# The bf16 split of the first attention's queries and keys on GpSimd and ScalarE in place of VectorE

## The reference, cut to what matters

```python
def qkv(h):
    t = (h @ qkv_W).reshape(b, n, 3, H, HD)          # H = 16 heads, HD = 8
    q, k, v = (t[:, :, 0], t[:, :, 1], t[:, :, 2])
    return (_apply_rope(q, cos, sin), _apply_rope(k, cos, sin), v)
...
s = jnp.einsum('bqhd,bkhd->bhqk', q, k) * scale
s = jnp.where(mask, s, jnp.finfo(s.dtype).min)
a = jax.nn.softmax(s, axis=-1)
return jnp.einsum('bhqk,bkhd->bqhd', a, v)
```

## Time and profile before

| | before |
|---|---|
| median of 3 runs | 969.55 us (968.15 to 973.97) |
| the profiled execution | 973.68 us |
| its span, first to last instruction | 971.8 us |
| TensorE busy | 909.4 us, 94% of the span |
| VectorE busy | 704.0 us, 72% |
| ScalarE busy | 550.3 us, 57% |
| GpSimd busy | 147.1 us, 15% |
| mean granted TensorE clock | 0.973 of full speed |

### The profile page before, as it was taken

The page is one execution under the profiler, slowest core; times in us unless marked ns, Lnnn a source line. Parts: engine busy times, 40 slices in busy tenths (PEclk is TensorE's granted clock), DMA queues, the critical chain, the costliest instruction groups (busy, mean ns, idle before and its releaser), DMA issues.

```text
span 971.8 us, 15418 instructions
## 1 busy us (share of the span) xinstructions
PE 909.4 (94%) x4959; PEld 396.5 (41%) x4986; DVE 704.0 (72%) x1933; ACT 550.3 (57%) x1033; POOL 147.1 (15%) x388
## 2 busy tenths in 40 slices
PE   3858999999999999999999999999899999999998
PEld 3523344334434345444444544434333334334443
DVE  5598958978887758643464667798599898886752
ACT  5023565465555566683437362377576676676773
POOL 1013200003000022210111120022001102021210
PEclk9877999999999999999999999999899999999999
DMA  8042131012311202000020224012422140004201
GB/s 312 29 134 66 54 110 29 18 42 75 86 59 49 60 3 69 3 8 1 1 66 7 66 91 111 7 56 80 103 66 60 46 115 24 3 3 135 81 3 33
DMA packets 66323, 57.49 MB, mean 59 GB/s; under 512 B 19407, under 2 KB 63427, under 8 KB 65988
## 3 DMA queue, kind: packets, MB, share of 16 engines
q1 hardware_dynamic: 64996, 54.73, 19.6%
q10 hardware_dynamic: 1248, 1.77, 0.5%
HBM read 31.01 MB, written 24.49 MB: 57 GB/s over the span
## 4 chain that ended last, share of the span: by engine, by line
PE 80%; DVE 12%; issue 3%; ACT 2%; DMA 1%; POOL 0%; SPq 0%; ACTq 0%; DVEq 0%
PE pv_bank L1540 15%; PE bank L1518 11%; PE bank L1495 10%; PE bank L1520 5%; PE bank L1522 4%; DVE bank L1271 3%; PE bank L1651 3%; PE bank L1646 3%; PE bank L1498 3%; PE bank L1633 3%; PE bank L1599 2%; PE bank L1600 2%; PE bank L1565 2%; PE bank L1506 2%; PE bank L1468 2%
## 5 line engine op out<-in xcount | busy, mean ns | idle before, releaser
L1019 ACT ACTIVATE pr<-bank 128x512 f32<-128x512 f32 (+1 forms) x704 | 371.3, 600 | 148.4 <-PE bank L1520 56.9
L1271 DVE CUSTOM_DVE_ANT_0 bank<-bank,mask_q 128x512 f32<-128x512 f32 x256 | 170.5, 718 | 24.6 <-PE bank L1495 23.3
L1274 DVE TENSOR_REDUCE mx<-bank 128x1 f32<-128x512 f32 x256 | 161.8, 684 | 32.9 <-PE bank L1495 32.3
L1518 PE MATMUL bank<-qs,ks 103*128 103x512 bf16 x512 | 178.6, 387 | 4.5 <-DMA qs<-mrow 2.3
L1495 PE MATMUL bank<-ks,qs 97*128 97x512 bf16 x512 | 166.2, 394 | 10.0 <-issue 7.5
L1540 PE MATMUL pv_bank<-pr,va 128*32 128x512 f32 x1024 | 137.3, 608 | 0.2
L1276 DVE TENSOR_REDUCE mx<-bank 128x4 f32<-128x308 f32 x192 | 81.5, 469 | 19.1 <-PE bank L1498 18.3
L915 POOL CAST mp<-mx 128x16 bf16<-128x16 f32 x80 | 16.4, 205 | 516.0 <-DVE mx L1271 203.5
L1518 PEld LDWEIGHTS bank<-qs,ks 103*128 103x128 bf16 x512 | 46.5, 98 | 117.3 <-ACT pr L1019 39.5
L1520 PE MATMUL bank<-mask_k,identb 128*128 128x512 bf16 x229 | 87.6, 383 | 0.0
L1495 PEld LDWEIGHTS bank<-ks,qs 97*128 97x128 bf16 x512 | 47.3, 99 | 98.8 <-issue 29.6
(11 more groups left out here) (219 smaller groups left out, 1186.8 us busy)
## 6 DMA issues: line engine op xcount, KB each, us to landing
qs<-q_parts SPq DMA_DIRECT2D x40, 384.0 KB, 4.6
q_parts<-xn SPq DMA_DIRECT2D x20, 384.0 KB, 2.6
ks<-k_parts SPq DMA_DIRECT2D x64, 96.0 KB, 2.6
q_parts<-xn SPq DMA_DIRECT2D x20, 256.0 KB, 2.2
k_parts<-u SPq DMA_DIRECT2D x8, 384.0 KB, 2.4
q_parts<-u SPq DMA_DIRECT2D x20, 128.0 KB, 2.1
qs<-mrow SPq DMA_DIRECT2D x160, 6.0 KB
late<-late_w SPq DMA_DIRECT2D x1, 2432.0 KB, 13.0
```

The lines of the kernel that those rows point to most:

```text
L1019: act.activation(pr[0:K, 4 * (group % NSLOT) + t % 4, :], bank(k)[0:K, :], ACT.Exp, scale=SCALE).then_inc(act_done, 1)
L1271: dve.tensor_tensor_reduce(b[:, :], b[:, :], mask_q[:, qb, :], 1.0, -3e38, ALU.add, ALU.max, dst[:, qb, g, e:e + 1]).then_inc(dve_done, 1)
L1274: dve.tensor_reduce(dst[:, qb, g, e:e + 1], b[:, :], AX.X, ALU.max).then_inc(dve_done, 1)
L1518: ins = pe.matmul(b[:, :], ks[s][0:ROWS, e, g, kb * P:(kb + 1) * P], qs[s][0:ROWS, g, :], start=True, stop=(a != 0))
```

## The change: what is done where

For attention 0 the one step `parts` on VectorE becomes three steps: `rest` on GpSimd (q - part 1 into `r1`), `second` on ScalarE (cast of `r1` to part 2), `third` on GpSimd (`r1` - part 2 into part 3). `parts_out` waits for `third`. Every step that writes into `hid` (VectorE's `rope` and `parts`, ScalarE's `proj` of layer 1, `gate_h`, `mlp_h`) now also waits for the last `third` ahead of it in the plan. The other attentions keep their `parts`. The scheduler knows the new steps and their holds, and its bonuses have other values, so the whole order is another one. The core of the diff:

```diff
-    "part1": ("act",), "parts": ("dve",), "part1_out": ...
+    "part1": ("act",), "parts": ("dve",), "rest": ("pool",), "second": ("act",), "third": ("pool",), "part1_out": ...
 def split(s, a, w):
     return (of(s, ("part1", a, w)) + (of(s, ("part1_out", a)) if w == 0 else [])
-            + of(s, ("parts", a, w), ("parts_out", a, w)))
+            + of(s, ("rest", a, w), ("second", a, w), ("third", a, w), ("parts_out", a, w)))
...
-TABLE_LOAD, TABLE_KEPT = 1.3, -143.9017
+TABLE_LOAD, TABLE_KEPT = 1.3, -149.7069
...
-EAGER = {"chain": 0.401623, "rows": 0.078331, "max": 0.046568, "exp": 0.072625, "pv": -0.094903, "tables": 0.309366}
+EAGER = {"chain": 0.401744, "rows": 0.045653, "max": 0.045471, "exp": 0.141877, "pv": -0.093953, "tables": 0.155199}
...
+                def rest(k, s, a, w):
+                    pool.wait_ge(act_done, count("act", (s, "part1", a, w)))
+                    pool.tensor_tensor(r1[w][s][:, :], qf[w][s][:, :], qpart(w, s, 0), ALU.subtract).then_inc(pool_done, 1)
+
+                def third(k, s, a, w):
+                    pool.wait_ge(act_done, count("act", (s, "second", a, w)))
+                    pool.wait_ge(pool_done, count("pool", (s, "rest", a, w)))
+                    pool.tensor_tensor(qpart(w, s, 2), r1[w][s][:, :], qpart(w, s, 1), ALU.subtract).then_inc(pool_done, 1)
...
+                def second(k, s, a, w):
+                    act.wait_ge(pool_done, count("pool", (s, "rest", a, w)))
+                    act.activation(qpart(w, s, 1), r1[w][s][:, :], ACT.Identity).then_inc(act_done, 1)
...
                     reader = before_in_plan(k, None, "parts")
                     if reader:
                         dve.wait_ge(dve_done, count("dve", reader))
+                    turned = before_in_plan(k, None, "third")
+                    if turned:
+                        dve.wait_ge(pool_done, count("pool", turned))
...
-                    if a == 0:
-                        dve.wait_ge(act_done, count("act", (s, "part1", a, w)))
-                        do(dve.tensor_tensor(rest, qf[w][s][:, :], part[0], ALU.subtract))
```

More of the change, by code:

```diff
@@ L90 @@
     "rope": ("pe", "dve"), "proj": ("pe", "act"), "v": ("pe", "act"),
-    "part1": ("act",), "parts": ("dve",), "part1_out": ("sp",), "parts_out": ("sp",), "stack": ("sp",),
+    "part1": ("act",), "parts": ("dve",), "rest": ("pool",), "second": ("act",), "third": ("pool",), "part1_out": ("sp",), "parts_out": ("sp",), "stack": ("sp",),
     "max": ("pe", "dve"), "max_parts": ("pool",), "max_t": ("pe", "dve"), "max_rows": ("sp",),
@@ L211 @@
          "ln_stats": (1.45,), "ln_rstd": (1.05,), "ln_norm": (1.07,), "ctx_stats": (2.,), "ln_t": (.44, .7),
-         "ctx_norm": (2.5,), "rope": (.86, .82), "part1": (.56,), "parts": (1.85,), "v": (.89, .6), "ctx_t": (.25, .7),
+         "ctx_norm": (2.5,), "rope": (.86, .82), "part1": (.56,), "rest": (1.3,), "second": (.56,), "third": (1.3,), "parts": (1.85,), "v": (.89, .6), "ctx_t": (.25, .7),
          "ctx_k": (.8, .8), "gate_cols": (.3,), "ctx_v": (.88, 1.9), "gates": (.4, .5), "ctx_split": (1.62,), "max_parts": (1.1,),
@@ L333, in before @@
             return [me("act", "ln_t", MLP_LN[rest[0]])], []
+        if kind == "rest":
+            return [me("act", "part1", *rest)], []
+        if kind == "second":
+            return [me("pool", "rest", *rest)], []
+        if kind == "third":
+            return [me("act", "second", *rest)], []
+        if kind == "parts_out":
+            return [me("dve", "parts", *rest) if rest[0] else me("pool", "third", *rest)], []
         if kind in ("part1", "part1_out", "parts"):
@@ L361, in before @@
                   "ln_rstd": ("dve", "ln_stats", *rest), "ln_norm": ("pool", "ln_rstd", *rest),
-                  "parts_out": ("dve", "parts", *rest),
                   "heads_t": ("act", "pv_out", *rest), "attn_t": ("dve", "heads_t", *rest, 1),
@@ L498 @@
 SIMPLE = {"e2_out", "gates", "ctx_k", "ctx_v", "ctx_split", "ctx_out", "ln_rstd", "ln_norm",
-          "parts_out", "heads_t", "attn_t", "mlp_out", "mlp_add", "l1_exp", "l1_probs", "l1_probs_t", "l1_evidence",
+          "heads_t", "attn_t", "mlp_out", "mlp_add", "l1_exp", "l1_probs", "l1_probs_t", "l1_evidence",
           "router", "router_exp", "router_probs", "probs_t", "gate_h", "expert_h", "gate", "l1_add", "store"}
@@ L839, in parts_out @@
                 def parts_out(k, s, a, w):
-                    sp.wait_ge(dve_done, count("dve", (s, "parts", a, w)))
+                    if a == 0:
+                        sp.wait_ge(pool_done, count("pool", (s, "third", a, w)))
+                    else:
+                        sp.wait_ge(dve_done, count("dve", (s, "parts", a, w)))
                     if w == 0:
@@ L998, in hid_free @@
                         act.wait_ge(dve_done, count("dve", reader))
+                    turned = before_in_plan(k, None, "third")
+                    if turned:
+                        act.wait_ge(pool_done, count("pool", turned))
                 def proj(k, s, a, w):
@@ L1248, in parts @@
                         dve.wait_ge(dve_done, count("dve", reader))
-                    if a == 0:
-                        dve.wait_ge(act_done, count("act", (s, "part1", a, w)))
-                        do(dve.tensor_tensor(rest, qf[w][s][:, :], part[0], ALU.subtract))
-                    else:
-                        first = (s, "proj", a, w)
-                        dve.wait_ge(act_done, count("act", first))
-                        b = 0.0 if QBIAS[a] is None else cols[:, QBIAS[a] + w:QBIAS[a] + w + 1]
-                        do(dve.scalar_tensor_tensor(rest, bank(first)[:, :], b, part[0], ALU.add, ALU.subtract))
+                    turned = before_in_plan(k, None, "third")
+                    if turned:
+                        dve.wait_ge(pool_done, count("pool", turned))
+                    first = (s, "proj", a, w)
+                    dve.wait_ge(act_done, count("act", first))
+                    b = 0.0 if QBIAS[a] is None else cols[:, QBIAS[a] + w:QBIAS[a] + w + 1]
+                    do(dve.scalar_tensor_tensor(rest, bank(first)[:, :], b, part[0], ALU.add, ALU.subtract))
                     do(dve.tensor_copy(part[1], rest))
```

4 lines of the change are left out of this document (2 added, 2 removed), and 6 rows, old and new, of the table URGE.

## The result

The changed kernel takes 977.61 us (median of 18 runs, 974.98 to 980.83), the kernel before 971.56 in the same comparison (18 runs, 967.51 to 977.61). The ratio is 1.006, 95% interval 1.0045 to 1.0075: about 6 us slower, where I had forecast 3.2 us faster. The measured time lies just above my range.

What follows compares the result with a forecast made beforehand. TensorE was taken as the bound, 98% busy from 100 to 575 us, with VectorE busiest in the ramp. Ramp gains of 0.3, 1.9 and 1 us made 3.2: 969.55 to 966.3 us, range 957 to 976.

Steps and rivals of the forecast that it cites:

- The prices of the parts: Eight splits: VectorE loses 14.6 us; each GpSimd pass takes 1.28 us, the ScalarE cast 0.63.
- the 78 to 83: Sign of being right, in the ramp: the first `exp` starts at 78 to 83 us.
- my 25.7: Ramp: the way from the first `max` matmul, laid out at 55.6 us, to the first `exp` at 81.3.
- 31 said: Sign of being right: TensorE idle about 31 us in the first 100 us.
- the rival of the held queue: `rope` waiting for `third` holds VectorE's queue, 1.6 us at eight places: 12.8 us, result 982; chance 0.07.
- mutual blocking as I priced it: Rival: all 16 GpSimd passes hit a VectorE instruction at 0.95 us, 15.2 less the 3.2: 981.5; chance 0.05.
- VectorE's time did not count in full: Judges the rival that VectorE, full in the ramp, gives back all 14.6 us: 955; chance 0.20.
- Behind 100 us I take zero: After the ramp: no gain or loss counted, though another order of later layers can add or save a few us.
- The last of my signs of being wrong: A difference that arises behind 100 us and is larger than that of the ramp.
- nothing to be seen: Rival: the ramp's gain is lost at a later place of the new order: 969.5; chance 0.18.
- The 3.2 us of the ramp: Total gain forecast from the start of the kernel: 3.2 us faster.
- the terms of 0.3, 1.9 and 1 us: Ramp: earlier first `exp` 0.3; context keys, values and gates done before it 1.9; maxima running ahead 1.

Runs made afterwards that it cites:

- e5: Step order of the kernel before, with the eight splits on GpSimd and ScalarE, each begun right behind part 1; 0.9993 to the kernel before.
- e2: The changed kernel's step order, with the eight splits put back on VectorE; 1.0053 to the kernel before.
- e14: The changed kernel, order untouched, lane 2's first 16 masked maxima run over half the keys (part of the computation left out); 1.0049 to the kernel before.
- e6: The changed kernel, with GpSimd's 3.51 us memsets for lanes 1 and 2 moved from `ctx_norm` to the start; 1.0085 to the kernel before.
- e10: The changed kernel's engines, lane 0's k rope right behind its q rope, a newly searched order behind it; 1.0018 to the kernel before.
- e12: Kernel before's order with new engines and early splits, first 149 steps rewritten so lane 0's k rope follows its q rope; 0.9822, median 953.45 us.
- e8: The changed kernel, lane 0's last row of maxima moved ahead, two groups of lane 1 and 2 steps placed later; 1.0048 to the kernel before.

## Why the prediction was wrong

**What held.** The prices of the parts: GpSimd's passes took 1.15 us (I had 1.28; my 1.2 to 1.4 lay just above), the cast 0.63, VectorE lost 14.0 us (14.6; its total of 690.0 lies in the 688 to 692). Two more signs came true by luck. The first `exp` at 82.66 lies in the 78 to 83, but only because the first `max` came 4.3 us later than I had laid out and the way from there took 22.7 us in place of my 25.7. TensorE's idle time in the first 100 us is 30.3 (31 said), but its matmuls were slower there, so that hardly more work was done (46.3 us lost against 46.7). VectorE waited for GpSimd ahead of no cos or sin product, so the rival of the held queue fell. So did that of mutual blocking as I priced it: GpSimd's 16 passes took 1151 to 1162 ns each, and of the VectorE instructions that ran beside one of them, mostly masked maxima (at most 733 ns), none was longer than its usual. None of the two products and the sum of a rope ever stood beside a pass, so of these the trace says nothing. VectorE's time did not count in full; it counted for nothing, as TensorE's 98% said. This much of the reading, that TensorE is the bound and eight splits off VectorE are worth little, fits e5.

**The step that failed** is "Behind 100 us I take zero". The hand-over at 140 us alone costs 5 to 6 us, and 300 to 575 us another 1 to 4. The last of my signs of being wrong, a difference that arises behind 100 us and is larger than that of the ramp, is what came. I had seen that the bonuses change and that the order behind the ramp is another, wrote that this can add or save a few of the 28 us of idle time, and gave it no term, no sign and no place. The order was there to be read: nine maxima of lane 2 ahead of lane 0's last one, and the last `exp` tiles of the group before issued among the first four of them. e2 shows that this order costs 0.5% with the old engines too. A last row costs about 8 us from its last maximum to the `exp` (135.9 to 144.1), and TensorE's list has 3.8 us less than that of other work at this place. The rival "nothing to be seen" had the mechanism (the gain lost at a later place of the new order) and stopped at zero, where nothing says that such a loss stops at the size of the gain.

**The 3.2 us of the ramp** were not there either in the profiled pair: 46.3 us lost in the first 100 against 46.7. I laid the start out with old durations. Lane 0's last `third` ends at 51.8, not 47.3, and the first `max` is at 59.9, not 55.6. 0.7 of these 4.3 us is `rstd`, 1.92 us in place of 1.0 since the mask cast now runs beside it:

```profile
22.90 1.22 DVE L1142 TENSOR_SCALAR mask_q<-qs 128x2048 bf16<-128x2048 uint8 x1
```

```profile
23.07 1.92 POOL L925 TENSOR_TENSOR rstd<-var,eps_pow 128x4 f32<-128x4 f32 x1 [18.84 <-DVE var L1241]
```

The rest is TensorE's pace: I had put the q rope's start at 29.7 and the anchors at 4.4 us, and they came out at 32.31 and 6.8, with 0.72 us for each pair of the bias rows. It need not be the order's doing. In e14, which has the same instructions in the same order up to there, the same matmuls ran faster:

```profile
27.96 0.51 PE L1417 MATMUL bank<-early,pr 128*128 128x128 f32 x2
...
32.30 1.62 PE L1425 MATMUL bank<-cond,pr 128*128 128x4 f32 x14
```

There the k rope starts at 37.09 in place of 42.78 and the first `exp` at 77.25 in place of 82.66. So a ramp laid out from one execution is uncertain by 5 us for this alone, and the terms of 0.3, 1.9 and 1 us in my sum were smaller than that. In e14 and e6 the first 100 us lose 40.5 and 43.7 us, 3 to 6 less than before: a gain of the size that I forecast does occur, in the traces whose clock first rises at 28.1 and 37.3 us in place of 47.2. Of the 5.4 us between their first `exp` the spans of e14 and the changed kernel keep at most 2 (974.1 against 976.1).

**The range** ended at 976, and the measured 977.61 is 1.6 above it. The median of before also went up, from 969.55 in the 3 runs that I had to 971.56 in 18; on my base the ratio of 1.006 gives 975.4. So that the number lies outside is due as much to the base as to the forecast, and that the range nearly held the slowdown is luck, as nothing in my sum provided for one. What was wrong is the sign. A term for one missed hand-over, about 6 us, belonged there; that idle time can cost clock as well could be seen in the earlier trace rows, 0.51 and 0.50 of full speed in the two stretches where TensorE was busy for 1.09 and 2.81 of 5 us.

## What to carry to other kernels

When an edit comes with a new schedule, they are two changes: freeze the old order around the new engines, and the new order around the old ones, before either gets the credit. Where one engine is full and its order fixed, follow the last producer of each group: see what stands ahead of it in every queue that it crosses, and how much work that is free to run the full engine has until the result arrives. A gain at the start is kept only if the order behind it is one that had been good; e10 and e12 have much the same early start (first `exp` at 66.7 and 68.0 us), and their medians are 972.7 and 953.5 us, 958.0 when e12 was run again.

## What the runs showed of the hardware that I had not expected

**Matmuls of one kind at two paces, by execution.** The same fp32 matmul pairs of the bias rows followed each other at 0.72 us in the changed kernel and at 0.42 in e14, with a granted clock of 1.00 shown for both stretches (28 to 32 us). In each trace the first record of the clock is its first rise: at 47.2 us in the changed kernel, 28.1 in e14, 31.2 in the kernel before. Until then the views show 1.00, and the matmuls run slowly: the anchors' pairs take 0.52 us in the changed kernel under a shown 1.00, just as in e14 under a shown 0.50 (from 35 us on). So at the start of an execution the granted clock in the rows does not tell the pace. Why the rise came so late in some executions the traces do not show. The Trainium skill, "TensorE: Matmul & The Clock Gate", section "What's actually happening", says that the number of slow matmuls at a start varies from run to run and costs less than 1% of a typical span. The two traces agree: they are 5.4 us apart at the first `exp`, of 976.

**Blocking does occur, but not at the maxima that I feared for.** A VectorE cast of 128x77 took 1.56 us beside GpSimd's memset (0.20 otherwise), and GpSimd's `rstd` 1.92 beside VectorE's mask cast (1.01 otherwise). Both VectorE instructions are `tensor_scalar` with one SBUF operand; the maxima, which read PSUM, were not slowed. The passes of the split can do it too, where the order puts them beside such a cast, as in e5:

```profile
51.35 1.16 POOL L944 TENSOR_TENSOR hid<-hid,u 128x512 f32<-128x512 f32 x1 [14.89 <-ACT u L1062]
51.57 0.99 DVE L1232 TENSOR_SCALAR cmaskf<-cmask 128x77 f32<-128x77 uint8 x1
```

And the collision of the earlier trace rows occurs again in the changed kernel, in a later attention, whose `parts` stay on VectorE (0.69 us otherwise):

```profile
590.97 1.32 POOL L950 TENSOR_TENSOR x<-x,bias_b 128x512 f32<-128x512 f32 x1
591.21 1.63 DVE L1287 TENSOR_TENSOR u<-hid,xn 128x512 bf16<-128x512 f32 x1
```

The Trainium skill, "SBUF — State Buffer", section "Who interferes with whom", names copies, casts and `tensor_scalar` as those that can take the ports shared with GpSimd, and says that whoever came first makes the other wait. The traces agree in both directions: in e8 the cast came behind the memset and waited, and at 23 us GpSimd's `rstd` started later and was the one that waited.
